# Column maxima by one-column stationaries on TensorE, bias rows made earlier, and new engine orders in a cross-attention + soft-MoE kernel

## The chip, the cores and the metric

One Trainium2 chip, one of its cores. The metric is device microseconds of one launch, the median of three runs. The engines are TensorE (PE, its weight loads shown as PEld), VectorE (DVE), ScalarE (ACT), GpSimd (POOL) and SyncE (SP), which issues all DMAs here.

## The reference

```
x   = x + xattn(layernorm(x), ctx, ctx, mask)          # 2x1024x256, 16 heads of 64, 154 keys
h   = layernorm(layernorm(x), norm_g, norm_b)
se  = layernorm(slot_embeds, slot_g, slot_b) * scale   # 16 experts x 64 slots = 1024 slots
logits   = einsum('bnd,esd->bnes', h, se)
dispatch = softmax(logits, axis=1)                     # over the 1024 tokens: column maxima
combine  = softmax(logits.reshape(B, N, -1), axis=-1)  # over the 1024 slots: row maxima
slots = einsum('bnd,bnes->besd', h, dispatch)
eout  = (gelu(slots @ Wg + bg) * (slots @ Wu + bu)) @ Wd + bd     # per expert, F = 512
x = x + einsum('bns,bso->bno', combine, eout)
```

All is float32. The kernel gets near this precision by splitting each operand into a "high" part of type fp32r and the rest, "low", and by summing three products (high·high, low·high, high·low).

## The kernel before

Each engine has its own list of events, and every list comes from one master order; the `LATER_*` tables move an event of one engine's list by so many places. PE follows the master order itself. The engines meet by semaphores only. Four stages follow one another: attention (0 to about 303 us), logits (to about 355), dispatch (to about 412) and experts (to about 508), then the combine.

**Logits.** For each of 16 tiles of 128 tokens: PE transposes the normed tile (`x2T`), ACT and DVE make its halves, PE multiplies with the slots (`L`, 12 matmuls), ACT copies the logits to SBUF (`lsb`), DVE keeps a running column maximum (`colmax`) and takes row maxima (`A`, `neg_amax`). For each batch b and half c, the column maxima are then brought to all rows: `MX` is four PE transposes of `colmax` and a DVE reduction to `nb`, whose column t holds the negated maxima of 128 slots, one a partition. DVE makes `diag`, four diagonal matrices (identity times `nb`, 128x512), and `MB` is one PE matmul ones·diag, a true float32 matmul that the trace shows as two records; DVE copies the result to `nb_b`.

**Dispatch.** For n = 0 to 15: POOL adds `nb_b` to the logits (`E`, into `disp_f` or `colmax`), ACT takes exp and the high half (`H`), DVE the low half, PE multiplies (`D`, 24 matmuls), DVE divides (`slot_f`), PE transposes (`sT`), and ACT and DVE make halves. Batch 0 has its maxima before the dispatch begins; batch 1's `MX` and `MB` stand at its opening.

**Weights.** Each expert has three pieces (0 gate, 1 up, 2 down), 512 KB each, in six places `w_raw`. ACT casts a piece to its high half (`W`, L786); POOL (L739) makes the low half of pieces 0 and 2, DVE (L983) that of piece 1. SP loads a piece into a place when the low half of the piece six before it has been made (L600).

**Experts.** For e: `GU` is 12 matmuls plus 2 that add bias rows from `b_row`; ACT takes gelu into `gate` and casts pieces 0 and 1 of expert e+2; DVE multiplies `hid` and makes the low half of piece (e+2, 1). `HT` is four PE transposes of `hid`, and ACT and DVE make `hT`. `EO` is 13 matmuls; DVE copies the result out as halves, and ACT casts piece 2. PE's order is GU(e+1), HT(e), EO(e-1), and a bank rule lets an accumulator be used again once DVE has freed the third one before it. `b_row` is cleared by DVE, filled by ACT (high) and DVE (low) between the last dispatch steps.

In the fences, the suffixed `wkq` and `w_second` are places that dispatch halves or weight halves use at that time.

## Time and profile before

| | |
|---|---|
| median of 3 runs | 572.33 us (571.97 to 572.97) |
| the profiled execution | 572.37 us, its span 570.6 us |
| PE busy | 537.8 us (94%) |
| DVE busy | 466.0 us (82%) |
| ACT busy | 395.1 us (69%) |
| POOL busy | 313.6 us (55%) |
| granted TensorE clock | 1.00 throughout |
| chain that ended last | PE 62%, DVE 16%, POOL 9%, ACT 7%, issue 6% |

Shares are averages over stages with different limits, so the table says only that PE is the main engine and that DVE stands in the chain for a sixth of the time. In a timeline row the number in brackets is how long the engine stood idle before it and who ended the wait. A row of several instructions is merged, so that its start and the next row's start give its pitch, while its own length has the last one's drain in it.

### The profile page before, as it was taken

The numbers are of one execution on the slowest core, as the hardware profiler recorded it, in microseconds if no ns is written. First come the engines' busy times: TensorE is split into PE (matmuls) and PEld (weight loads), VectorE is DVE, ScalarE is ACT, GpSimd is POOL, SyncE is SP. The second block draws the span as 40 slices with busy tenths as digits, with TensorE's granted clock in tenths as the row PEclk, the third lists the DMA queues.
The fourth block names the chain that finished last, engine by engine and source line by source line (L and its number), as shares of the span: only waits on it lengthen the run. The fifth ranks groups of instructions, "written<-read, shape, count | busy, mean of one in ns | idle before, by whom it ended". The sixth has DMA issues, their size and how long they took to land.

```text
span 570.6 us, 11928 instructions
## 1 busy us (share of the span) xinstructions
PE 537.8 (94%) x3877; PEld 499.5 (88%) x3877; DVE 466.0 (82%) x1354; ACT 395.1 (69%) x1073; POOL 313.6 (55%) x331
## 2 busy tenths in 40 slices
PE   5889999999999999999989998899979999999997
PEld 3778999999999989999977876799948787899997
DVE  7897878788797979898766997997788999985553
ACT  4976959698796959689663555578967676736662
POOL 7662554455445464453456766886498999920000
PEclk9999999999999999999999999999999999999999
DMA  8402000000030000000001433050268888516552
GB/s 262 169 1 75 2 2 2 1 2 1 2 93 2 2 2 0 3 1 2 1 2 74 184 149 148 38 191 18 82 204 277 273 284 271 180 38 184 167 169 73
DMA packets 29868, 51.78 MB, mean 91 GB/s; under 512 B 2037, under 2 KB 16465, under 8 KB 29681
## 3 DMA queue, kind: packets, MB, share of 16 engines
q1 hardware_dynamic: 29809, 51.04, 26.7%
q8 instruction: 32, 0.52, 0.4%
q14 instruction: 27, 0.22, 0.1%
HBM read 40.54 MB, written 10.49 MB: 89 GB/s over the span
## 4 chain that ended last, share of the span: by engine, by line
PE 62%; DVE 16%; POOL 9%; ACT 7%; issue 6%; DMA 0%; SPq 0%; POOLq 0%; ACTq 0%; DVEq 0%
PE ps L1453 8%; PE ps L1315 8%; PE ps L1516 7%; PE ps L1403 6%; PE ps L1485 6%; DVE w_gu_low L983 5%; PE ps L1436 5%; PE ps L1384 5%; PE ps L1415 4%; PE ps L1438 3%; PE ps L1575 2%; POOL prob L680 2%; ACT expo L828 2%; DVE eo_high L1263 1%; PE ps L1362 1%
## 5 line engine op out<-in xcount | busy, mean ns | idle before, releaser
L680 POOL TENSOR_TENSOR prob<-expo,prec 128x512 f32<-128x512 f32 x64 | 66.8, 1044 | 99.2 <-DVE prec L1100 97.9
L828 ACT ACTIVATE expo<-expo,nmin 128x154 f32<-128x154 f32 x256 | 106.2, 422 | 3.8 <-DVE nmin L1089 3.3
L1089 DVE CUSTOM_DVE_ANT_0 expo<-ps,maskb 128x154 f32<-128x154 f32 x256 | 69.1, 311 | 12.5 <-PE ps L1403 11.9
L1403 PE MATMUL ps<-kbd,qT_high 128*128 128x308 f32 x256 | 60.9, 321 | 0.3 <-ACT qT_high L754 0.3
L1109 DVE TENSOR_TENSOR pT_low<-ps,pT_high 128x512 fp32r<-128x512 f32 (+1 forms) x96 | 57.2, 595 | 4.1 <-ACT pT_high L842 3.6
L842 ACT CAST pT_high<-ps 128x512 fp32r<-128x512 f32 (+1 forms) x96 | 49.2, 515 | 15.2 <-PE ps L1415 11.5
L754 ACT ACTIVATE oT_high<-ps,bqv_c 128x256 fp32r<-128x256 f32 x64 | 29.9, 468 | 37.0 <-PE ps L1438 37.0
L828 ACT ACTIVATION_READ_ACCUMULATOR expo<-expo,nmin 128x1 f32 x256 | 50.1, 196 | 0.0
L739 POOL TENSOR_TENSOR wkq_low<-w_raw,wkq_high 128x1024 fp32r<-128x1024 f32 x15 | 48.1, 3208 | 1.5 <-ACT wkq_high L786 1.5
L739 POOL TENSOR_TENSOR w_gu_low<-w_raw,w_gu_high 128x1024 fp32r<-128x1024 f32 x17 | 41.8, 2465 | 11.8 <-ACT w_gu_high L786 11.8
L1403 PEld LDWEIGHTS ps<-kbd,qT_high 128*128 128x128 f32 x256 | 40.0, 190 | 0.9 <-issue 0.5
L983 DVE TENSOR_TENSOR w_gu_low<-w_raw,w_gu_high 128x1024 fp32r<-128x1024 f32 x14 | 37.6, 2683 | 2.7 <-ACT w_gu_high L786 2.7
L1403 PE MATMUL ps<-kbd,qT_low 128*128 128x308 f32 x128 | 39.0, 305 | 0.0
L1415 PE MATMUL ps<-ident,prob 128*128 128x128 f32 x256 | 38.4, 272 | 0.0
L1453 PE MATMUL ps<-wvo_high,oT_high 128*128 128x256 f32 x128 | 36.8, 287 | 0.0
L1453 PE MATMUL ps<-wvo_high,oT_low 128*128 128x256 f32 x128 | 36.2, 283 | 0.0
L1453 PE MATMUL ps<-wvo_low,oT_high 128*128 128x256 f32 x128 | 35.9, 281 | 0.0
L945 ACT CAST comb<-ps 128x512 fp32r<-128x512 f32 x32 | 17.3, 591 | 25.7 <-PE ps L1575 25.7
L971 DVE SCALAR_TENSOR_TENSOR oT_low<-ps,bqv_c,oT_high 128x256 fp32r<-128x256 f32 x64 | 30.4, 474 | 5.8 <-ACT oT_high L754 5.1
L1315 PE MATMUL ps<-eo_high,comb 128*128 128x256 f32 x256 | 34.6, 287 | 0.4 <-issue 0.4
L867 ACT COPY lsb<-ps 128x512 f32<-128x512 f32 x32 | 17.2, 589 | 25.2 <-PE ps L1485 25.2
L1315 PEld LDWEIGHTS ps<-eo_high,comb 128*128 128x128 f32 x256 | 31.7, 191 | 0.6 <-issue 0.6
(239 smaller groups left out, 1775.6 us busy)
## 6 DMA issues: line engine op xcount, KB each, us to landing
logits_dram<-lsb SPq DMA_DIRECT2D x16, 512.0 KB, 2.6
w_raw<-in_L_ffn_Wg_dram SPq DMA_DIRECT2D x16, 512.0 KB, 4.2
w_raw<-in_L_ffn_Wu_dram SPq DMA_DIRECT2D x16, 512.0 KB, 4.4
...
```

The lines of the kernel that those rows point to most:

```text
L680: pool.tensor_tensor(prob[:, n % 2, :, heads, :], expo[:, n % 2, pp, :, :, 0:P], prec[:, n % 2, pp].unsqueeze(3).to_broadcast([P, 2, 2, P] ...
L739: pool.tensor_tensor(low, w_raw[:, i % RAW].rearrange("p (k n) -> p k n", k=KD if w == 0 else FT), high, ALU.subtract).then_inc(low_made(e ...
L828: ins = act.activation(row, row, ACT.Exp, scale=-1.0, bias=nmin[:, n % 2, pp, j, h:h + 1], accum_out=psums[:, n % 2, pp, j, h:h + 1])
L842: act.copy(pT[0][0:rows, n % 2, 2 * t:2 * t + tiles], ps[0:rows, NS + k % NT, 0:tiles * 2 * P].rearrange("p (t n) -> p t n", t=tiles))\
L983: dve.tensor_tensor(low, w_raw[:, i % RAW].rearrange("p (k n) -> p k n", k=KD if w < 2 else FT), high, ALU.subtract).then_inc(low_made(e, ...
L1089: ins = dve.tensor_tensor_reduce(out=expo[:, n % 2, pp, j, h, :], in0=ps[:, s % NS, h * SK:(h + 1) * SK], in1=maskb[:, (2 * (n // QUADS) + ...
L1109: dve.tensor_tensor(pT[1][0:rows, n % 2, 2 * t:2 * t + tiles], ps[0:rows, NS + k % NT, 0:tiles * 2 * P].rearrange("p (t n) -> p t n", t=ti ...
L1315: ins = pe.matmul(dst[:, 0:D], combT[s][:, i % 2, t], eo[m][:, i // TB, t], start=(first and r == 0 and t == parts[0]), stop=(last and r = ...
L1403: ins = pe.matmul(dst, qT[s][:, n % 2, pp, j * P:(j + 1) * P], kbd[:, b, m, p, :], start=(r == 0), stop=(r == 2))
L1415: ins = pe.transpose(ps[:, NS + k % NT, (2 * h + j) * P:(2 * h + j + 1) * P], prob[:, n % 2, j, 2 * t + h, 0:P], ident[:])
L1453: ins = pe.matmul(dst[:, 0:D], oT[s][:, p, j * P:(j + 1) * P], wo[m][:, p], start=(p == 0 and r == 0), stop=(p == PAIRS - 1 and r == 2))
L1516: ins = pe.matmul(dst[:, 0:DN], disp[s][n % 3][:, i], x2[m][:, b * TB + i], start=(r == 0 and i == 0), stop=(r == 2 and i == TB - 1))
```

## The change

Four things:

1. `diag` and `ones` are gone. `MB` is four matmuls of 128 columns: the stationary is one column of `nb`, repeated 128 times by its access pattern, and the moving operand is the identity.
2. `b_row` has a place of its own in SBUF. POOL clears it in the logits; ACT and DVE fill it after step 9 of the dispatch, in place of its very end.
3. In the opening of the dispatch both transposes of batch 1 stand ahead of `D(0)`.
4. The tables that shift events are new, among them those of the experts.

The pieces of code below stand, in this order, on POOL (clearing `b_row`), on DVE (`MX`, then the event that cleared `b_row`) and on PE (`MB`).

```diff
-A_LATE = 4
+A_LATE = 3
-FIRST_AT = {9: [('C', 0)], 10: [('C', 1)], 11: [('C', 2)], 12: [('W', 0, 0)], 13: [('B', 0), ('W', 0, 1), ('gelu',)], 14: [('W', 0, 2), ('B', 1), ('W', 1, 2)]}
+FIRST_AT = {6: [('B', 1)], 9: [('C', 0)], 10: [('C', 2), ('C', 1)], 12: [('W', 0, 0)], 13: [('W', 0, 1), ('W', 0, 2), ('gelu',)], 14: [('W', 1, 2)]}
 SLOTS_HEAD = [
-    ("H", 0), ("MX", 1, 0), ("D", 0), ("H", 1), ("MX", 1, 1), ("MB", 1, 0),
+    ("H", 0), ("MX", 1, 0), ("MX", 1, 1), ("D", 0), ("H", 1), ("MB", 1, 0),
 ]
...
 LATER_EXPERTS_DVE = {
-    "HT": -2, "GU": -1, "C": -0.5,
+    "HT": -2, "C": -0.5, ("EO", 2): -1,
 }
...
-    b_row = sb(ex, "b_row", [P, BW], F32R)
+    b_row = nc.alloc_sbuf_tensor_at("b_row", [P, BW], F32R, offset=b_row_at)
...
+            elif ev == ("B", 0):
+                pool.wait_ge(acc_free, ATT_END)
+                pool.memset(b_row[:].bitcast(F32), 0.0).then_inc(b_zeros, 1)
...
-                part_nb = nb[:, 4 * c:4 * c + 4]
-                dve.tensor_reduce(part_nb, acc(no).rearrange("p (t n) -> p t n", t=4), AX, ALU.max, negate=True)\
-                    .then_inc(acc_free, 1)
-                wait_used(dve, ev)
-                dve.tensor_tensor(diag[:], ident[:].unsqueeze(1).to_broadcast([P, 4, P]),
-                                  part_nb.unsqueeze(2).to_broadcast([P, 4, P]), ALU.mult).then_inc(diag_ready, 1)
+                dve.tensor_reduce(nb[:, 4 * c:4 * c + 4], acc(no).rearrange("p (t n) -> p t n", t=4), AX, ALU.max,
+                                  negate=True).then_inc(acc_free, 1)
...
-                dve.wait_ge(d_shift, B * ST)
-                dve.wait_ge(d_lst, 16 * TILES)
-                dve.memset(b_row[:].bitcast(F32), 0.0)
...
-                pe.wait_ge(diag_ready, 2 * b + c + 1)
-                pe.matmul(dst, ones[:], diag[:].rearrange("p t n -> p (t n)"), start=True, stop=True)\
-                    .then_inc(acc_full, 1)
+                wait_used(pe, ("MX", b, c))
+                for t in range(4):
+                    ins = pe.matmul(dst[:, t * P:(t + 1) * P], nb[:, 4 * c + t:4 * c + t + 1].to_broadcast([P, P]),
+                                    ident[:], start=True, stop=True)
+                ins.then_inc(acc_full, 1)
```

DVE where the dispatch opens, from the low half of step 0 on; before:

```order
L1215 TENSOR_TENSOR disp_low<-disp_f_62,disp_high 128x1024
L1200 TENSOR_REDUCE nb<-ps 128x4
L1203 TENSOR_TENSOR diag<-ident,nb 128x512
L1221 RECIPROCAL den<-ps 128x1
L1222 TENSOR_SCALAR slot_f<-ps,den 128x256
L1215 TENSOR_TENSOR wkq_low<-ps,wkq_high 128x1024
L1200 TENSOR_REDUCE nb<-ps 128x4
L1203 TENSOR_TENSOR diag<-ident,nb 128x512
L1208 COPY nb_b<-ps 128x512
```

The same place of DVE now:

```order
L1214 TENSOR_TENSOR disp_low<-disp_f_62,disp_high 128x1024
L1202 TENSOR_REDUCE nb<-ps 128x4 x2
L1220 RECIPROCAL den<-ps 128x1
L1221 TENSOR_SCALAR slot_f<-ps,den 128x256
L1214 TENSOR_TENSOR wkq_low<-ps,wkq_high 128x1024
L1207 COPY nb_b<-ps 128x512
```

Both reductions now stand ahead of step 0's division, and nothing stands between a reduction and what PE waits for.

DVE in the experts, one period and the start of the next; before:

```order
L1250 TENSOR_TENSOR hid<-ps,gate 128x512
L983 TENSOR_TENSOR w_gu_low<-w_raw,w_gu_high 128x1024
L969 TENSOR_TENSOR hT_low<-ps,hT_high 128x512
L1263 CAST eo_high<-ps 64x256 x2
L1266 TENSOR_TENSOR eo_low<-ps,eo_high 64x256 x2
L1250 TENSOR_TENSOR hid<-ps,gate 128x512
```

The same place now:

```order
L973 TENSOR_TENSOR hT_low<-ps,hT_high 128x512
L1247 TENSOR_TENSOR hid<-ps,gate 128x512
L986 TENSOR_TENSOR w_gu_low<-w_raw,w_gu_high 128x1024
L1260 CAST eo_high<-ps 64x256 x2
L1263 TENSOR_TENSOR eo_low<-ps,eo_high 64x256 x2
L973 TENSOR_TENSOR hT_low<-ps,hT_high 128x512
```

`hT_low(e-1)` now precedes `hid(e)` and the weight half; it followed both.

ACT at the end of the dispatch, from step 13's halves of slots on; before:

```order
L893 CAST sT_high<-ps 128x2x64 x2
L902 ACT_TABLE_LOAD
L902 ACTIVATE csum<-csum 128x1
L786 CAST wkq_high<-w_raw 128x1024
L893 CAST sT_high<-ps 128x2x64 x2
L906 CAST b_row<-b_raw 16x1280
L786 CAST wkq_high<-w_raw 128x1024
L786 CAST w_second_high<-w_raw 128x1024 x2
```

The same place now, with the cast of piece (0, 2) in the first row:

```order
L790 CAST wkq_high<-w_raw 128x1024
L897 CAST sT_high<-ps 128x2x64 x2
L906 ACT_TABLE_LOAD
L906 ACTIVATE csum<-csum 128x1
L790 CAST wkq_high<-w_raw 128x1024
L897 CAST sT_high<-ps 128x2x64 x2
L790 CAST w_second_high<-w_raw 128x1024 x2
```

The bias cast has left this place, and the two down pieces come one place earlier each.

## Rows read from the trace of the kernel before

**Rows 1.** Windows: length, then busy us of PE, PEld, DVE, ACT, POOL, clock, DMA.

```profile
368.00:412.00 44.00, 44.00 (x368) 43.92 (x367) 36.94 (x80) 36.66 (x63) 27.62 (x13) 1.00 0.25 86
...
436.00:494.00 58.00, 55.59 (x316) 46.75 (x316) 56.58 (x71) 40.69 (x53) 58.00 (x21) 1.00 0.84 271
```

**Rows 2.** Timeline of PE where the dispatch opens: start, us, instruction, [idle before <-releaser].

```profile
361.99 1.10 PE L1502 MATMUL ps<-diag,ones 128*128 128x512 f32 x2 [0.90 <-DVE diag L1203]
...
367.12 1.10 PE L1502 MATMUL ps<-diag,ones 128*128 128x512 f32 x2 [1.15 <-DVE diag L1203]
```

**Rows 3.** Timeline of DVE: `diag` in the logits, then where the dispatch opens.

```profile
333.32 0.69 DVE L1203 TENSOR_TENSOR diag<-ident,nb 128x512 f32<-128x512 f32 x1
...
359.37 2.47 DVE L1203 TENSOR_TENSOR diag<-ident,nb 128x512 f32<-128x512 f32 x1
...
364.20 2.77 DVE L1203 TENSOR_TENSOR diag<-ident,nb 128x512 f32<-128x512 f32 x1
```

**Rows 4.** Timeline of POOL where the dispatch opens.

```profile
358.90 5.17 POOL L728 TENSOR_TENSOR disp_f<-lsb,nb_b 128x1024 f32<-128x1024 f32 x2 [1.25 <-DVE disp_low L1215]
364.03 2.39 POOL L728 TENSOR_TENSOR colmax<-lsb,nb_b 128x1024 f32<-128x1024 f32 x1
```

**Rows 5.** Timeline of PE in the logits.

```profile
337.29 1.02 PE L1502 MATMUL ps<-diag,ones 128*128 128x512 f32 x2
338.15 0.38 PE L1469 MATMUL ps<-ident,x2f 128*128 128x128 f32 x2
...
345.25 0.72 PE L1485 MATMUL ps<-wkq_high,x2T_high 128*128 128x512 f32 x2 [0.28 <-DVE x2T_low L969]
```

**Rows 6.** Timeline of PE from expert 0 to the first combine.

```profile
415.78 0.73 PE L1546 MATMUL ps<-b_row,b_pick 128*128 128x512 f32 x2 [0.94 <-DVE b_row L1243]
...
419.12 0.73 PE L1541 MATMUL ps<-w_second_low,sT_high 128*128 128x512 f32 x2 [1.46 <-DVE w_second_low L983]
...
428.77 0.36 PE L1560 MATMUL ps<-b_row,b_pick 128*128 128x256 f32 x1 [1.06 <-DVE hT_low L969]
...
507.89 1.84 PE L1315 MATMUL ps<-eo_high,comb 128*128 128x256 f32 x14
```

**Rows 7.** Timeline of POOL at the start of the experts.

```profile
406.55 4.77 POOL L739 TENSOR_TENSOR w_gu_low<-w_raw,w_gu_high 128x1024 fp32r<-128x1024 f32 x2 [9.16 <-ACT w_gu_high L786]
...
414.72 3.26 POOL L739 TENSOR_TENSOR wkq_low<-w_raw,wkq_high 128x1024 fp32r<-128x1024 f32 x1 [0.34 <-ACT wkq_high L786]
417.94 3.37 POOL L739 TENSOR_TENSOR w_second_low<-w_raw,w_second_high 128x1024 fp32r<-128x1024 f32 x1
```

**Rows 8.** Timeline of ACT and of DVE: the bias rows.

```profile
412.44 1.26 ACT L906 CAST b_row<-b_raw 16x1280 fp32r<-16x1280 f32 x1
...
414.15 1.58 DVE L1243 TENSOR_TENSOR b_row<-b_raw,b_row 16x1280 fp32r<-16x1280 f32 x1 [1.08 <-ACT b_row L906]
```

**Rows 9.** Timeline of DVE, one expert's period.

```profile
455.97 0.68 DVE L969 TENSOR_TENSOR hT_low<-ps,hT_high 128x512 fp32r<-128x512 f32 x1
...
458.33 0.69 DVE L1250 TENSOR_TENSOR hid<-ps,gate 128x512 f32<-128x512 f32 x1
458.94 2.82 DVE L983 TENSOR_TENSOR w_gu_low<-w_raw,w_gu_high 128x1024 fp32r<-128x1024 f32 x1
```

**Rows 10.** Timeline of POOL, the same period.

```profile
458.25 2.42 POOL L739 TENSOR_TENSOR w_gu_low<-w_raw,w_gu_high 128x1024 fp32r<-128x1024 f32 x1
460.62 3.40 POOL L739 TENSOR_TENSOR wkq_low<-w_raw,wkq_high 128x1024 fp32r<-128x1024 f32 x1
```

**Rows 11.** Timeline of PE, the same period.

```profile
456.74 0.36 PE L1560 MATMUL ps<-b_row,b_pick 128*128 128x256 f32 x1 [0.24 <-DVE hT_low L969]
```

**Rows 12.** Timeline of ACT, the same period.

```profile
456.10 0.60 ACT L912 ACTIVATE gate<-ps 128x512 f32<-128x512 f32 x1 [1.78 <-PE ps L1546]
...
458.49 0.60 ACT L754 ACTIVATE hT_high<-ps 128x512 fp32r<-128x512 f32 x1
```

**Rows 13.** Tile `w_raw` in the experts, last line of the answer.

```profile
DMA to landing us min/median/max: 3.2/4.2/5.9
```

More of the change, by code:

```diff
@@ L86 @@
 SLOTS_HEAD = [
-    ("H", 0), ("MX", 1, 0), ("D", 0), ("H", 1), ("MX", 1, 1), ("MB", 1, 0),
+    ("H", 0), ("MX", 1, 0), ("MX", 1, 1), ("D", 0), ("H", 1), ("MB", 1, 0),
 ]
-LOGITS_AT = {8: [('MX', 0, 0)], 10: [('MB', 0, 0)], 11: [('MX', 0, 1)], 13: [('E', 0), ('MB', 0, 1)], 14: [('E', 1)], 15: [('E', 2)]}
+LOGITS_AT = {3: [('B', 0)], 8: [('MX', 0, 0)], 10: [('MB', 0, 0)], 11: [('MX', 0, 1)], 13: [('E', 0), ('MB', 0, 1)], 14: [('E', 1)], 15: [('E', 2)]}
 LATER_SLOTS_ACT = {
     "GU": 3.5, ("E", 0): 4, ("E", 1): 4, ("E", 2): 7, "sT": 2, ("W", 0, 1): -0.5, ("E", 15): 1,
-    ("W", 1, 0): -1, ("GU", 1): 3, "E": 0.5, ("D", 1): 1, ("E", 14): 1.5,
+    ("W", 1, 0): -1, ("GU", 1): 3, "E": 0.5, ("D", 1): 1, ("E", 14): 1.5, ("E", 13): -1.5, ("W", 0, 2): -0.5,
 }
 LATER_SLOTS_DVE = {
-    "GU": 3.5, "L": 1, "A": 4, "E": -1, ("C", 2): 0.5, "H": 0.5, ("E", 15): 0.5, ("D", 1): -2, ("L", 13): 3,
-    ("W", 0, 2): -4, ("W", 0, 0): 4,
+    "GU": 3.5, "L": 1, "A": 4, "E": -3, ("C", 2): 0.5, "H": 0.5, ("E", 15): 0.5, ("D", 1): -2, ("L", 13): 3,
+    ("W", 0, 2): -4, ("W", 0, 0): 4, ("H", 3): 1.5, "x2T": -0.5, ("W", 1, 0): 1, ("E", 9): -2.5,
 }
 LATER_SLOTS_POOL = {
-    "E": 1.5, ("C", 0): 1, ("L", 14): -4, ("L", 13): 0.5, "L": 0.5, ("C", 1): 2, ("E", 8): 3.5, "MB": -1,
-    ("W", 0, 1): 0.5, ("E", 9): 0.5, ("E", 2): 0.5, ("H", 0): 1, ("H", 2): 1, ("GU", 1): -0.5,
[3 rows of a table added]
 }
 LATER_EXPERTS_ACT = {
-    "C": 2, ("EO", 14): -0.5,
+    "C": 2, ("EO", 14): -0.5, "CO": 2,
 }
 LATER_EXPERTS_DVE = {
-    "HT": -2, "GU": -1, "C": -0.5,
+    "HT": -2, "C": -0.5, ("EO", 2): -1,
 }
@@ L299, in program @@
     ident16 = sb(top, "ident16", [P, P], BF16)
-    ones = sb(top, "ones", [P, P])
     x1 = sb(top, "x1", [P, TILES, D])
@@ L379, in program @@
     nb = sb(lg, "nb", [P, ST])
-    diag = sb(lg, "diag", [P, 4, P])
     slot_f = sb(lg, "slot_f", [P, 2, D])
+    b_row_at = -(-nc.sbuf_base // 32) * 32
     lg.close()
@@ L469, in program @@
     l_full, l_ready, amax_ready, colmax_ready = sem("l_full"), sem("l_ready"), sem("amax_ready"), sem("colmax_ready")
-    diag_ready = sem("diag_ready")
     d_shift, d_exp, d_high, d_low = (sem(s) for s in ("d_shift", "d_exp", "d_high", "d_low"))
+    b_pick_ready, b_zeros = sem("b_pick_ready"), sem("b_zeros")
     w_high, gate_low, up_low, down_low, b_high, b_low = (sem(s) for s in (
@@ L904, in step @@
                 act.wait_ge(d_bias, 48)
-                act.wait_ge(const_dve, 3)
+                act.wait_ge(b_zeros, 1)
                 act.copy(b_row[0:E], b_raw[:]).then_inc(b_high, 1)
@@ L974, in _ @@
         dve.memset(eps[:], EPS)
-        dve.memset(mhalf[:], -0.5)
-        dve.memset(ones[:], 1.0).then_inc(const_dve, 1)
+        dve.memset(mhalf[:], -0.5).then_inc(const_dve, 1)
         def weight_low(e, w):
@@ L1195, in step @@
                 wait_done(dve, ev)
-                if (b, c) != (0, 0):
-                    wait_done(dve, ("MB", (2 * b + c - 1) // 2, (c + 1) % 2))
-                part_nb = nb[:, 4 * c:4 * c + 4]
-                dve.tensor_reduce(part_nb, acc(no).rearrange("p (t n) -> p t n", t=4), AX, ALU.max, negate=True)\
-                    .then_inc(acc_free, 1)
-                wait_used(dve, ev)
-                dve.tensor_tensor(diag[:], ident[:].unsqueeze(1).to_broadcast([P, 4, P]),
-                                  part_nb.unsqueeze(2).to_broadcast([P, 4, P]), ALU.mult).then_inc(diag_ready, 1)
+                if b:
+                    wait_done(dve, ("MB", 0, c))
+                dve.tensor_reduce(nb[:, 4 * c:4 * c + 4], acc(no).rearrange("p (t n) -> p t n", t=4), AX, ALU.max,
+                                  negate=True).then_inc(acc_free, 1)
             elif ev[0] == "MB":
@@ L1234, in step @@
             elif ev == ("B", 0):
-                dve.wait_ge(d_shift, B * ST)
-                dve.wait_ge(d_lst, 16 * TILES)
-                dve.memset(b_row[:].bitcast(F32), 0.0)
-                dve.tensor_tensor(b_pick[:], ident[:, 0:E], ident[:, 32:32 + E], ALU.add).then_inc(const_dve, 1)
+                dve.wait_ge(se_ready, ST)
+                dve.tensor_tensor(b_pick[:], ident[:, 0:E], ident[:, 32:32 + E], ALU.add).then_inc(b_pick_ready, 1)
             elif ev == ("B", 1):
-                dve.wait_ge(const_dve, 3)
+                dve.wait_ge(b_pick_ready, 1)
+                dve.wait_ge(b_zeros, 1)
                 dve.wait_ge(b_high, 1)
```

3 rows, old and new, of the table LATER_SLOTS_POOL are left out of this document.

## The prediction

> **What bounds the kernel now.** I read the chain that ended last first, then the windows stage by stage, then the timelines of all engines where PE stands idle. In the dispatch PE is busy for 44.00 of 44 us [rows 1], so a microsecond won before it goes straight through it. In the experts PE is busy for 55.59 of 58, DVE for 56.58 and POOL for 58.00 of 58: POOL never rests [rows 1]. One period there is 5.7 us: 2.36 from `hT_low` to `hid`, 0.61 to the weight half, 2.74 until the next `hT_low` can start [rows 9].
>
> Where the time of DVE's weight half goes is seen by laying DVE over POOL. It starts at 458.94 while POOL is in an instruction that ends at 460.62; DVE ends at 461.76, 1.13 after that boundary, and POOL's next one takes 3.40 instead of 2.42, 0.98 more [rows 9, 10]. So the two take turns by whole instructions: DVE waits for POOL's boundary, then POOL waits 1.1. `diag` shows the same: 0.69 alone, 2.47 and 2.77 beside POOL [rows 3], the last ending 0.6 after POOL's boundary at 366.4 [rows 4]. The Trainium skill says it in "SBUF — State Buffer", section "SBUF: two separate sides": whichever of a two-SBUF-input DVE operation and a GpSimd operation starts first keeps the shared port pair for its whole length. By that rule, the rows agree.
>
> Hence a period of two POOL lows and one DVE low is 2.37 + 2.22 + 1.13 = 5.7 in whatever order DVE does its list, and DVE's own wait is elastic. What the order does set is how far behind that beat PE runs. Before, PE's `EO` waits for `hT_low`, which stands behind the weight half: 0.24 us idle each period [rows 11].
>
> **The change part by part.** The sum is made on the profiled execution: span 570.6 us, 572.37 in all, 0.04 above the median of the runs.
>
> *Opening.* PE waits 0.90 and 1.15 us for `diag` [rows 2]. Now `MB` needs only `nb`. Both transposes are done before `D(0)`, both reductions of 0.7 us pass while `D(0)` runs for 3 us, and both `MB`s find `nb` ready. What is late next is step 1's low half on DVE, about 363.2, wanted in the third pass of `D(1)` at 364. It fits. Gain 2.05; at least 0.9 if only one wait goes.
>
> *MB itself.* The old one streams 512 columns in two records, 337.29 to 338.15, 0.86 us [rows 5]. The new one streams the same columns in eight pieces of 128. Below: 0.86, or somewhat less if the access pattern helps, which nothing shows. Above: the record of two 128-column transposes is 0.38 long, 0.19 each [rows 5]; eight unhidden ones would be 1.52, 0.66 more. All four `MB`s lie on PE's path, so the cost is between 0 and 2.6. I take 0.05 each, 0.2, since the columns stream alike and weight loads pass beside matmuls elsewhere here.
>
> *Logits.* Two `diag`s of 0.7 us leave a DVE that is nearly full; PE's wait of 0.28 goes [rows 5], and a part of the issue time around it. Gain 0.3 to 0.6; I take 0.4. POOL's clearing of `b_row`: DVE's took 1.1 us and POOL's of kbd is alike; it stands while POOL would wait for ACT, and delays `x2f` by about 0.5 with 1.5 to spare. Nothing; 0.5 at most if that cover is gone. The dispatch thus starts 2.05 + 0.4 − 0.2 = 2.25 us earlier.
>
> *Inside the dispatch.* ACT gets the bias cast, 1.26, DVE the subtraction, 1.58 [rows 8]. The windows leave ACT 7.3 and DVE 7.1 us idle in 44 [rows 1], the halves are made 2 to 3 us ahead of their matmuls in the middle, and the gap closes again before the end. The subtraction has two SBUF inputs, so it can wait for POOL's instruction of 2.4 us [rows 4], 4 in all; that still fits. DVE no longer has the fourth late row maximum. Cost 0 taken. At the end ACT's list is dense (three combine exps, E(13) to E(15), pieces): high halves 13 and 15 come only 0.2 and 0.6 us ahead. Bounds −0 to +2.5.
>
> *From dispatch to experts.* POOL makes the first lows: 406.55 for two, then one, then 3.26 and 3.37, ending at 421.3 [rows 7]. Three things stretch that: waits for ACT's casts, the subtraction of `b_row` (1.58, rows 8), and DVE's weight half. Now ACT has no bias cast there and both down pieces are cast earlier; the subtraction is gone. POOL starts at about 404.5 and makes five lows at 2.4 with one turn for DVE: 404.5 + 11.9 + 1.1 = 417.5, 3.8 earlier. PE's waits of 0.94 (bias) goes [rows 6], and those for POOL's lows in experts 1 and 2 remain, with their ends 3.7 earlier.
>
> *DVE's new order.* `hT_low(0)` no longer stands behind a weight half, so `EO(0)` starts at about 423.9, not 428.77 [rows 6]: 4.9 earlier. Call X the end of DVE's weight half in expert e. Then DVE copies `EO` (1.76), makes `hT_low` (0.6) and `hid` (0.7): `hid` is ready at X + 3.1, and the next request waits for POOL, X + 5.7. PE now waits in `HT(e)` for `hid`, and not in `EO`. The new wait of DVE is `hT_low` for ACT: gelu starts 456.10 and `hT_high` ends 459.09, 3.0 later [rows 12]; gelu can start with `hid`, X + 3.1, so `hT_high` is there at X + 6.1 and is wanted at X + 5.7 + 1.8 = X + 7.5. Slack 1.4. Queued behind that wait are `hid`, the weight half and the copies of `EO`, for which PE waits.
>
> Laid out by these durations, X is 424.5, 430.9, 436.6 for pieces (3,1), (4,1), (5,1), then every 5.7 us, the tenth later at 493.6. The old last one is at 496.0. So the beat is 2.3 to 2.4 earlier, and PE stands nearly 3 us nearer to it than before, which makes `EO(3)` 5.1 earlier. The end gives part of that back: `HT(15)` needs `hid(15)`, behind two copies of `EO` and one `hT_low` more: 493.6 + 1.8 + 0.6 + 0.7 + 1.8 + 0.6 + 0.7 = 499.8. From there `HT`, half a combine transpose, `EO(14)`, `EO(15)` are 4.1 us, so the first combine starts at 503.9 and not at 507.89 [rows 6]: 4.0 earlier, 4.2 if the dispatch has the full 2.25.
>
> *Combine.* Nothing in it is moved. **Sum:** 572.37 − 4.2 = 568.2 us; against the median, 568.1.
>
> **The rivals.**
>
> A. *PE breaks away from the beat.* If ACT's cast of piece (2,2) is a little later than I have it (0.35 us between POOL's start and DVE's request), DVE gets its turn one POOL instruction earlier. The beat is then 2 us earlier from expert 2 on. For: the margin is small. Against: POOL is full and has the same work. 568.1 − 2.2 = 565.9.
>
> B. *Only the opening pays.* PE stays tied to POOL's stream, which in the end hangs on ACT's casts and on the loads: `GU` and `EO` wait for POOL's halves in place of DVE's. For: POOL 58.00 of 58 [rows 1]. Against: its halves are done about 4 us before PE needs them. Gain 2.25 and some 0.3: 569.8.
>
> C. *The dispatch gets crowded, or `MB` is dear.* High halves 12 to 15 each late by 0.5 (2.0), or the upper bound of `MB`. For: 0.2 us of slack. 570.4.
>
> D. *Slower: `hid` behind ACT.* DVE now does nothing until ACT has cast two pieces, and these wait for loads. A load may start when DVE's low half two experts earlier is made, and takes 4.2 in the median, 5.9 at most [rows 13]. I have piece (6,1) land only 0.25 us before its cast. It decides from a landing of 4.4 + 0.25 + 1.4, about 6 us: then `hT_high` comes after X + 7.5, DVE misses POOL's boundary, and a period costs 0.5 more. Eleven such periods are 5.5, less 4.2: 573.6. For: PE runs earlier than its data did before, while the places `w_raw` are as many. Against: only the longest landing seen reaches it.
>
> E. *It doesn't do what it says.* If repeated columns as stationary ran at a slower pace than any row here, `MB` could cost back the 2.05; that ends at 570 to 572.5 and shares C's chance.
>
> **How the numbers follow.** Forecast 0.50, its own range 566.8 to 569.3. A 0.15, B 0.14, C with E 0.13, D 0.08. The measurement tells about 0.2%, 1.1 us, from no change: faster is below 571.2. Faster: all of the forecast, A and B, and most of C: 0.86. Same: the rest of C, and D where half the periods are late: 0.07. Slower 0.07. The range for 8 in 10 is 565.5 to 571.0; it has the forecast, A, B and C, and leaves out D and the tails.
>
> **What would show it.** Opening: no idle before the two `MB`s, each 0.85 to 1.0 us, and the dispatch's first steady step 2.0 to 2.5 us earlier. DVE: `nb` rows of 0.7, no two-input operation in the opening besides step 0's. Transition: POOL's five lows without a gap, ending near 417.5; no wait of PE for `b_row`. Experts: period 5.7, POOL full; PE's idle of 0.2 to 0.4 before `HT` (waiting for `hid`), none before `EO`. First combine near 503.9. I am wrong if `MB` takes 1.2 or more, if PE waits in the dispatch for `disp_high` or `wkq_high`, if the period isn't 5.7, or if DVE's idle before `hT_low` grows over the 1.4 of slack.

## The result and the profile after

| | before | changed | ratio, 95% interval |
|---|---|---|---|
| first chip | 572.44 us (571.97 to 572.97, 4 runs) | 567.46 us (567.09 to 569.12, 4 runs) | 0.9918 [0.9906, 0.993] |
| a later chip, the changed kernel again | 572.2 us (572.11 to 573.18, 11 runs) | 568.19 us (567.08 to 569.55, 6 runs) | 0.9927 [0.9915, 0.9938] |

The forecast was 568.1 us with a range of 565.5 to 571.0. The profiled execution took 567.2 us, its span is 565.4, 5.2 less than before. The page gives PE 537.4 us busy (95%), DVE 453.9, ACT 395.7, POOL 312.7, and the chain of what ended last:

```profile
PE 62%; DVE 14%; POOL 10%; ACT 7%; issue 5%; DMA 2%; SPq 1%; POOLq 0%; ACTq 0%; DVEq 0%
```

DVE's share fell from 16 to 14%, and there is a new 2% of DMA, of which more below. The windows that answer to [rows 1], with the same columns:

```profile
368.00:412.00 44.00, 44.00 (x363) 43.70 (x363) 35.59 (x79) 39.32 (x67) 28.79 (x13) 1.00 0.29 95
436.00:494.00 58.00, 56.09 (x324) 47.29 (x324) 56.37 (x75) 41.14 (x52) 56.76 (x20) 1.00 0.79 260
```

PE is still busy in all of the dispatch. In the experts POOL is no longer at 58.00 of 58. PE has 0.5 us more here, but that belongs to one event of this execution (told below); a second profile of the same kernel, without it, has 55.24:

```profile
436.00:494.00 58.00, 55.24 (x316) 45.84 (x315) 56.87 (x73) 39.56 (x51) 56.72 (x21) 1.00 0.75 256
```

**Opening.** PE's timeline, which answers to [rows 2]; the waits for `diag` are gone, and nothing stands before either `MB`:

```profile
356.48 1.91 PE L1491 MATMUL ps<-ident,colmax 128*128 128x128 f32 x8 [2.16 <-DVE colmax L1189]
358.04 2.05 PE L1515 MATMUL ps<-x_high,disp_high 128*128 128x258 f32 x8
359.90 1.15 PE L1515 MATMUL ps<-x_low,disp_high 128*128 128x258 f32 x8
...
361.86 1.05 PE L1500 MATMUL ps<-ident,nb 128*128 128x128 f32 x8
...
365.62 1.05 PE L1500 MATMUL ps<-ident,nb 128*128 128x128 f32 x8
...
366.65 1.21 PE L1515 MATMUL ps<-x_high,wkq_high 128*128 128x258 f32 x8
```

From the first transposes of batch 1 to `D(2)` it is 10.17 us; before it was 11.10 (357.12 to 368.22). That is 0.93 less, not the 2.05 of the forecast. The reason is in the pitch (the time from one group's start to the next one's): eight matmuls of `D(0)` take 1.86 us (358.04 to 359.90), and other groups of eight about 1.0. The windows of this stretch (clock in the third column from the end) say why:

```profile
350.00:356.40 6.40, 4.32 (x19) 3.17 (x17) 3.40 (x6) 4.08 (x7) 6.40 (x4) 1.00 0.35 145
356.40:358.00 1.60, 1.52 (x8) 1.55 (x9) 1.59 (x1) 1.51 (x2) 0.62 (x1) 0.54 0.74 300
358.00:359.80 1.80, 1.80 (x10) 1.80 (x9) 1.30 (x3) 1.71 (x3) 1.53 (x1) 0.50 0.00 0
```

After the idle 2.16 us in front of the transposes the granted clock is at half, that is 1.2 GHz, until `D(0)`'s first eight matmuls are through, and then it goes back to 2.4 GHz (0.97 in the mean from 359.80 to 362.00). Before had 1.00 there, although the idle 2.16 us is the same. A second profile of the changed kernel (span 566.2) had 1.00 throughout, and the same stretch, 357.06 to 365.65, takes 8.59 us:

```profile
357.06 1.07 PE L1491 MATMUL ps<-ident,colmax 128*128 128x128 f32 x8 [2.16 <-DVE colmax L1189]
...
365.65 1.20 PE L1515 MATMUL ps<-x_high,wkq_high 128*128 128x258 f32 x8
```

**From dispatch to experts.** POOL's timeline, which answers to [rows 7]. Five low halves without a gap, the last ending at 417.63 (before 421.27); from the start of the first it is 12.79 us, before 14.72:

```profile
404.84 4.76 POOL L743 TENSOR_TENSOR w_gu_low<-w_raw,w_gu_high 128x1024 fp32r<-128x1024 f32 x2 [9.11 <-ACT w_gu_high L790]
409.56 4.77 POOL L743 TENSOR_TENSOR wkq_low<-w_raw,wkq_high 128x1024 fp32r<-128x1024 f32 x2
414.30 3.38 POOL L743 TENSOR_TENSOR w_second_low<-w_raw,w_second_high 128x1024 fp32r<-128x1024 f32 x1
417.63 5.74 POOL L743 TENSOR_TENSOR w_gu_low<-w_raw,w_gu_high 128x1024 fp32r<-128x1024 f32 x2
```

**To the combine.** PE's timeline, which answers to [rows 6]. No wait for `b_row`, and the first `EO` at 423.83 without one; the first combine is 5.13 earlier than 507.89:

```profile
415.48 0.74 PE L1540 MATMUL ps<-w_second_low,sT_high 128*128 128x512 f32 x2 [0.66 <-DVE w_second_low L986]
...
421.06 0.73 PE L1540 MATMUL ps<-w_gu_low,sT_high 128*128 128x512 f32 x2 [0.77 <-POOL w_gu_low L743]
...
423.83 0.36 PE L1559 MATMUL ps<-b_row,b_pick 128*128 128x256 f32 x1
...
502.76 1.82 PE L1312 MATMUL ps<-eo_high,comb 128*128 128x256 f32 x14
```

**One period** of DVE, which answers to [rows 9], and the PE row of it, which answers to [rows 11]: PE now waits for `hid`, in `HT`, and `hT_low` is ahead of `hid`.

```profile
438.67 0.69 DVE L973 TENSOR_TENSOR hT_low<-ps,hT_high 128x512 fp32r<-128x512 f32 x1
439.27 0.68 DVE L1247 TENSOR_TENSOR hid<-ps,gate 128x512 f32<-128x512 f32 x1
439.87 2.67 DVE L986 TENSOR_TENSOR w_gu_low<-w_raw,w_gu_high 128x1024 fp32r<-128x1024 f32 x1
```

```profile
440.10 0.63 PE L1552 MATMUL ps<-ident,hid 128*128 128x128 f32 x4 [0.38 <-DVE hid L1247]
```

In that run one thing more happened, at 450. ACT's cast of a down piece waited 1.75 us for its load, POOL waited 0.97 for that cast, and DVE, which asked in just that gap, made its weight half at once, in 1.22 us. In the two periods before it had taken 2.67 and 2.80, and in the next it took 2.38:

```profile
451.26 1.22 DVE L986 TENSOR_TENSOR w_gu_low<-w_raw,w_gu_high 128x1024 fp32r<-128x1024 f32 x1
```

```profile
450.34 1.05 ACT L790 CAST wkq_high<-w_raw 128x1024 fp32r<-128x1024 f32 x1 [1.75 <-DMA w_raw<-in_L_ffn_Wd_dram]
```

```profile
451.47 3.29 POOL L743 TENSOR_TENSOR wkq_low<-w_raw,wkq_high 128x1024 fp32r<-128x1024 f32 x1 [0.97 <-ACT wkq_high L790]
```

From there all is 1.4 us ahead of the beat (the rhythm of 5.7 us). Call this a slip. The second profile has none, and from the end of POOL's five lows to the first combine it needs 86.50 us (416.61 to 503.11) where the first needs 85.13. The first profile thus holds a loss of about 1.6 (the clock) and a gain of about 1.4 (the slip), which hide each other. The table cuts the span of each profile into stretches that add up to it. The first row, all work ahead of the second logits tile, is not touched by the change, and yet it differs from one execution to another.

| us, profiled executions | before | changed, first | changed, second |
|---|---|---|---|
| start to the transposes of the second logits tile | 302.58 | 302.71 | 303.26 |
| from there to the first transposes of batch 1 (logits) | 54.54 | 53.77 | 53.80 |
| first transposes of batch 1 to `D(2)` | 11.10 | 10.17 | 8.59 |
| `D(2)` to POOL's first low half | 38.33 | 38.19 | 38.17 |
| five low halves | 14.72 | 12.79 | 12.79 |
| from there to the first combine | 86.62 | 85.13 | 86.50 |
| first combine to the end of the span | 62.71 | 62.64 | 63.09 |
| span | 570.6 | 565.4 | 566.2 |

### The profile page after: what moved, and what is told of

It is laid out like the page before. It is cut to its first block, busy times and chain, and to the rows that moved or that the text cites. A ratio compares the mean times of both kernels' runs of the same rounds, so it can differ in the third digit from the quotient of the medians.

```text
span 565.4 us, 11969 instructions
## 1 busy us (share of the span) xinstructions
PE 537.4 (95%) x3901; PEld 502.5 (89%) x3901; DVE 453.9 (80%) x1348; ACT 395.7 (70%) x1073; POOL 312.7 (55%) x332
## 4 chain that ended last, share of the span: by engine, by line
PE 62%; DVE 14%; POOL 10%; ACT 7%; issue 5%; DMA 2%; SPq 1%; POOLq 0%; ACTq 0%; DVEq 0%
PE ps L1450 8%; PE ps L1312 8%; PE ps L1482 7%; PE ps L1515 6%; PE ps L1400 6%; DVE w_gu_low L986 5%; PE ps L1433 5%; PE ps L1381 5%; PE ps L1412 4%; PE ps L1435 3%; PE ps L1574 2%; POOL prob L680 2%; ACT expo L832 2%; DVE eo_high L1260 2%; POOL w_gu_low L743 1%
## 5 line engine op out<-in xcount | busy, mean ns | idle before, releaser
L743 POOL TENSOR_TENSOR w_gu_low<-w_raw,w_gu_high 128x1024 fp32r<-128x1024 f32 x17 | 44.7, 2632 | 11.8 <-ACT w_gu_high L790 11.7
L743 POOL TENSOR_TENSOR wkq_low<-w_raw,wkq_high 128x1024 fp32r<-128x1024 f32 x15 | 43.8, 2924 | 1.0 <-ACT wkq_high L790 1.0
L986 DVE TENSOR_TENSOR w_gu_low<-w_raw,w_gu_high 128x1024 fp32r<-128x1024 f32 x14 | 34.1, 2435 | 0.0
```

The costliest lines, as they stand in the source:

```text
L743: pool.tensor_tensor(low, w_raw[:, i % RAW].rearrange("p (k n) -> p k n", k=KD if w == 0 else FT), high, ALU.subtract).then_inc(low_made(e ...
L986: dve.tensor_tensor(low, w_raw[:, i % RAW].rearrange("p (k n) -> p k n", k=KD if w < 2 else FT), high, ALU.subtract).then_inc(low_made(e, ...
```

## The experiments

Each kernel was timed beside the kernel before on its chip; ratios are against that. Three chips were used for the experiments, and the kernel before had medians of 572.93 (experiments 1 to 4), 572.57 (5 to 8) and 572.2 (9 to 12).

### 1 and 2. DVE's new order in the experts, alone and undone

The kernel before with only this table changed, and the changed kernel with the old one:

```diff
 LATER_EXPERTS_DVE = {
-    "HT": -2, "GU": -1, "C": -0.5,
+    "HT": -2, "C": -0.5, ("EO", 2): -1,
 }
```

> The kernel before, with one edit: the new table of DVE's events in the experts (hT_low(e-1) ahead of hid(e) and the weight half). Theory T (POOL and DVE take turns by whole instructions, the period is 5.7 us in any order, and DVE's order sets only how far behind that beat PE runs): PE's wait moves from EO to HT and PE comes closer to the beat, the end gives part back; 1.0 to 2.0 us faster than before, period still 5.7. Rival R (the experts gained only because POOL's first five low halves came earlier; DVE's order is worth nothing): within 0.3 us of before. Rival D (hid stands behind ACT's casts): slower by 1 us or more.

> The changed kernel, with DVE's old table in the experts. T: EO waits for hT_low behind the weight half again, 1.0 to 2.0 us slower than the changed kernel (about 569), period 5.7, POOL's first five lows as early as in the changed kernel. R: within 0.3 us of the changed kernel (567.5).

Alone it measured 572.26 us (571.96 to 573.1, 11 runs), ratio 0.9994 [0.9985, 1.0003]; undone, 567.57 (567.22 to 568.61, 4 runs), 0.9913 [0.9899, 0.9926]. So the order is worth nothing that can be measured, and the expectation of 1 to 2 us fell. The traces say why. In experiment 1 the last weight half of DVE ends at 497.21, 1.24 later than the old 495.97, since one item more stands ahead of it; but the first combine comes 10.30 us behind that and not 11.92:

```profile
507.51 1.84 PE L1315 MATMUL ps<-eo_high,comb 128*128 128x256 f32 x14
```

From POOL's five lows to the combine it takes 86.51 with the new order and 86.62 with the old; on top of the rest of the change it is 86.50 (second profile) and 86.66 (experiment 2). PE is nearer to DVE's beat, and the end gives it back.

Experiment 1's trace also tells what the fall of the clock costs the kernel before. Here it fell too (windows of PE's opening):

```profile
356.80:359.00 2.20, 2.10 (x10) 2.14 (x11) 2.18 (x2) 2.11 (x3) 0.94 (x2) 0.52 0.55 222
359.00:361.00 2.00, 2.00 (x14) 2.00 (x13) 1.97 (x2) 1.76 (x2) 2.00 (x1) 0.67 0.00 0
```

```profile
362.22 1.02 PE L1502 MATMUL ps<-diag,ones 128*128 128x512 f32 x2
...
366.91 1.10 PE L1502 MATMUL ps<-diag,ones 128*128 128x512 f32 x2 [0.78 <-DVE diag L1203]
...
368.01 1.22 PE L1516 MATMUL ps<-x_high,wkq_high 128*128 128x258 f32 x8
```

The first `MB` no longer waits for `diag` and the second waits 0.78. From the first transposes to `D(2)` it is 11.12 us with the fall, and 11.10 in the profile of before, without it. The old kernel's waits for DVE take up what the slow matmuls lose. The 1.31 us of `D(1)`'s first pass here (362.73 to 364.04) stands behind an `MB` that waited for nothing; it will matter in experiment 3.

### 3. The one-column `MB` alone

The kernel before with the new `MX` and `MB` on PE and DVE, all tables old:

```diff
-                pe.matmul(dst, ones[:], diag[:].rearrange("p t n -> p (t n)"), start=True, stop=True)\
-                    .then_inc(acc_full, 1)
+                for t in range(4):
+                    ins = pe.matmul(dst[:, t * P:(t + 1) * P], nb[:, 4 * c + t:4 * c + t + 1].to_broadcast([P, P]),
+                                    ident[:], start=True, stop=True)
+                ins.then_inc(acc_full, 1)
```

> The kernel before, with only the column maxima done by one-column stationaries (no diag, no ones; all orders as before). T: the two waits of 0.90 and 1.15 us at the opening mostly go, MB takes 0.89 instead of 0.86; but MX(1,1) still stands behind D(0), so a part of a wait stays, and PE may lose some clock there; 1.0 to 2.5 us faster than before. Rival (diag was hidden, the gain at the opening came from the new order of MX): under 0.5 us.

569.92 us (569.48 to 570.67, 5 runs), ratio 0.9955 [0.9941, 0.9969]: 3.0 us less, more than the 1.0 to 2.5 expected. The profile had 1.00 throughout: 8.62 us from the first transposes to `D(2)` (357.13 to 365.75), 2.48 less than before. The brackets of the two waits were 2.05 of it. Most of the rest is that a wait costs PE more than its bracket, since the bracket begins when the last matmul in front has drained, and without a wait the next one starts before that. From the second transposes to the first `MB` it was 1.51 us and is 0.43, 1.08 less for a bracket of 0.90; from the third pass of `D(1)` to the second `MB` it was 2.27 (364.85 to 367.12) and is 0.98, 1.29 less for a bracket of 1.15. The rows of before, and those of this run (where the transposes' row is 0.60 us long, too, but `MB` starts 0.43 behind their start):

```profile
360.48 0.60 PE L1494 MATMUL ps<-ident,colmax 128*128 128x128 f32 x4
```

```profile
360.48 0.60 PE L1490 MATMUL ps<-ident,colmax 128*128 128x128 f32 x4
360.91 1.06 PE L1499 MATMUL ps<-ident,nb 128*128 128x128 f32 x8
```

The matmuls behind the waits were not slower. `MB` and the first pass of `D(1)` together take 1.89 us before (361.99 to 363.88), 1.82 in experiment 1, where nothing waited in front of them, and 1.86 here.

The logits, too, are 0.75 us shorter: 53.79 us from the second tile's transposes (303.34) to the first of batch 1, against 54.54. Most of it lies in front of the two `MB`s there. The second one in the kernel before, from the transposes ahead of it:

```profile
344.59 0.38 PE L1469 MATMUL ps<-ident,x2f 128*128 128x128 f32 x2
...
348.15 1.02 PE L1502 MATMUL ps<-diag,ones 128*128 128x512 f32 x2
```

and here:

```profile
345.12 0.38 PE L1465 MATMUL ps<-ident,x2f 128*128 128x128 f32 x2
...
348.12 1.05 PE L1499 MATMUL ps<-ident,nb 128*128 128x128 f32 x8
```

That is 3.56 and 3.00 us; for the first one it is 3.30 (333.99 to 337.29) and 3.00 (334.78 to 337.78). What follows `D(2)` is as before.

### 4. The bias rows at their old place

```diff
-FIRST_AT = {6: [('B', 1)], 9: [('C', 0)], ... 14: [('W', 1, 2)]}
+FIRST_AT = {9: [('C', 0)], ... 14: [('B', 1), ('W', 1, 2)]}
```

> The changed kernel, with the bias rows' cast (ACT) and subtraction (DVE) put back to the end of the dispatch, ahead of the cast of piece (1,2); b_row is still cleared by POOL in the logits. T: ACT's later casts come 1.2 us later and the subtraction takes a turn of 1.4 us from POOL, so POOL's first five lows end 1.5 to 2.5 us later and PE waits for them; 1.0 to 2.5 us slower than the changed kernel (568.5 to 570). Rival (the bias rows were covered, what made POOL's lows earlier was the earlier dispatch alone): within 0.3 us of 567.5.

569.59 us (568.6 to 569.9, 5 runs), ratio 0.9941 [0.9929, 0.9954], in the expected 568.5 to 570. POOL's second down piece waits 0.28 us for ACT and takes 3.33 where it takes 2.4 in the changed kernel; the five lows take 14.01 us instead of 12.79, and from POOL's first low to the first combine it is 100.53 us where experiments 7 and 8 have 99.27 and 99.29:

```profile
412.04 3.33 POOL L743 TENSOR_TENSOR wkq_low<-w_raw,wkq_high 128x1024 fp32r<-128x1024 f32 x1 [0.28 <-ACT wkq_high L790]
```

```profile
413.16 0.73 PE L1545 MATMUL ps<-b_row,b_pick 128*128 128x512 f32 x2 [0.16 <-DVE b_row L1240]
```

The wait for `b_row` itself is 0.16 us. So it is not that wait that made the bias rows dear, but what ACT's cast and DVE's subtraction did to POOL's chain.

### 5 and 12. Matmuls in the wait

The changed kernel with nine matmuls of 512 bf16 columns, whose result nobody reads, in PE's wait before the first transposes of batch 1:

```diff
+                if (b, c) == (1, 0):
+                    for _ in range(9):
+                        pe.matmul(ps[:, 4, :], ident16[:], ident16[:].unsqueeze(1).to_broadcast([P, 4, P]),
+                                  start=True, stop=True)
                 pe.wait_ge(colmax_ready, TB * (b + 1))
```

> The changed kernel, with nine 128x512 bf16 matmuls into an unused bank right after the last logits matmul, in the 2.16 us in which PE waits for the last colmax; their result is never read. In the changed kernel's profile the transposes and the first pass of D(0) behind this wait ran at a lower clock (8 transposes in 1.56 us, 8 matmuls in 1.86 us instead of about 1.0). Theory C (the clock fell because PE stood idle for 2.16 us): no slow stretch, 1.0 to 1.6 us faster than the changed kernel (about 566.2). Rival (a disturbance of that one execution, or not caused by the wait): same as the changed kernel, 567.5.

> The changed kernel with nine filler matmuls in the wait before the first transposes of batch 1, the same as before, beside the changed kernel on one chip. If the idle 2.16 us brings the fall of the clock, all of its runs have a mean clock of 1.000 and the median is 0.5 to 1.5 us below the changed kernel's. If the fall is chance and not that wait, some of its runs have 0.997 as well and the medians are within 0.3.

566.93 us (566.79 to 567.47, 4 runs), ratio 0.9905 [0.989, 0.992], and on another chip, beside the changed kernel, 566.93 (566.82 to 567.48, 4 runs), 0.9905 [0.9892, 0.9918].

```profile
354.07 2.12 PE L1491 MATMUL ps<-ident 128*128 128x512 bf16 x9
356.30 1.09 PE L1495 MATMUL ps<-ident,colmax 128*128 128x128 f32 x8
```

On one chip it is 1.3 us below the changed kernel's 568.19; against the first chip's 567.46 it is 0.5, less than the 1.0 to 1.6 that were expected.

All 8 runs had a mean clock of 1.000. A mean of 0.996 or 0.997 is what the profiles have in which the clock fell at this place (the first of the changed kernel, experiments 1, 4, 6, 7 and 8), and it is counted as that fall in the other runs. Of the changed kernel's 10 runs on both chips 3 had 1.000 and 7 had 0.996 or 0.997; of the kernel before it was 21 of 35. So the idle 2.16 us is what lets the clock fall, in about two thirds of the runs of either kernel.

The price is read best from the traces. From the first transposes of batch 1 to `D(2)` it is 10.10 to 10.17 us in the five profiles of the new opening with the fall (the first of the changed kernel, experiments 4, 6, 7 and 8) and 8.59 to 8.63 in four without it (the second of the changed kernel, experiments 2, 5 and 12), so the fall costs the new opening about 1.5 us. The spans of whole runs show it less sharply, since the work ahead of the logits ends 1.1 us earlier or later from one profile to another (302.35 to 303.45): kernel by kernel, the mean span of the runs with the fall is longer by 0.7 us (the changed kernel, 566.5 against 565.9) to 1.6 (experiment 7). In the old opening it costs nothing that can be told: 570.98 against 570.73 in the kernel before, and in experiment 1 the 8 runs with it are 0.4 us shorter in the mean than the 3 without.

### 6. No turns between POOL and DVE

DVE's up-weight low halves from expert 2 on are replaced by a memset of the same size; the low part of these weights is thus left out of the result.

```diff
                 if e + 2 < E:
-                    weight_low(e + 2, 1)
+                    dve.wait_ge(w_high, i + 1)
+                    dve.memset(low.bitcast(F32), 0.0).then_inc(low_made(e + 2, 1)[0], 1)
```

> The changed kernel, where for experts 2 to 15 DVE's low half of the up weights is left out and a memset of the same place to zero stands for it, so that DVE has no operation with two SBUF inputs there (the low part of Wu is missing from the result). Theory T (DVE and POOL take turns): each POOL low takes 2.4 us, none 3.3; POOL has rests, the period is PE's own 5.3 to 5.5 us, PE hardly waits for hid; 2.5 to 4.5 us faster than the changed kernel (about 564). Rival (POOL's 3.3 us lows come from the DMA traffic or from what they write, not from DVE): POOL's lows stay at 3.3, period 5.7, gain under 1 us.

562.04 us (561.47 to 562.6, 4 runs), ratio 0.9817 [0.9803, 0.983]: 5.4 below the changed kernel's 567.46, more than the 2.5 to 4.5 expected (the changed kernel was not timed on this chip). All of POOL's low halves from expert 2 on take 2.4 us, and PE has no idle time left:

```profile
461.80 2.42 POOL L743 TENSOR_TENSOR w_gu_low<-w_raw,w_gu_high 128x1024 fp32r<-128x1024 f32 x1 [0.45 <-ACT w_gu_high L790]
```

```profile
436.00:490.00 54.00, 54.00 (x320) 47.16 (x319) 39.81 (x75) 40.34 (x52) 49.69 (x21) 1.00 0.84 275
```

The period is 5.22 us and no longer 5.70. What paces the experts is the turns, worth 6.0 us from the five lows to the combine (80.49 against 86.50; the memset is also 0.2 us shorter than the 1.13 of the subtraction it stands for), and behind them stands PE itself. A memset by DVE, without an SBUF input, made nobody wait.

### 7. The old tables of the logits and the dispatch

```diff
-A_LATE = 3
+A_LATE = 4
```

and the three `LATER_SLOTS_*` tables as before.

> The changed kernel, with the old tables of shifts for ACT, DVE and POOL from the logits to the first experts and A_LATE = 4; the places of the events in the master order are the new ones. T (in the dispatch PE bounds, so these shifts are covered but for the first casts of weights): slower than the changed kernel by 0 to 0.8 us (567.5 to 568.3). Rival (the searched shifts bring a good part of the gain): slower by over 1.5 us (569 or more).

568.36 us (566.83 to 568.76, 5 runs), ratio 0.9923 [0.991, 0.9935]. In its profile the clock fell too, and the three rows of the table above from the first transposes of batch 1 to the end of the five low halves are 10.13, 38.42 and 12.77 us, against 10.17, 38.19 and 12.79. The new tables bring 0.2 us, in the dispatch. The median, just over the expected 567.5 to 568.3, says no more than that, since four of the five runs had the fall.

### 8. The second transposes behind `D(0)` again

```diff
-    ("H", 0), ("MX", 1, 0), ("MX", 1, 1), ("D", 0), ("H", 1), ("MB", 1, 0),
+    ("H", 0), ("MX", 1, 0), ("D", 0), ("H", 1), ("MX", 1, 1), ("MB", 1, 0),
```

> The changed kernel, with MX(1,1) behind D(0) again. T: DVE's division of step 0 and low half of step 1 stand before its second reduction; MB(1,1) still finds nb ready, since it comes 3 us after; within 0.3 us of the changed kernel (567.5). Rival (the new place is needed): 0.5 to 1.2 us slower.

568.41 us (567.59 to 569.04, 5 runs), ratio 0.9928 [0.9916, 0.994]. By the number alone the rival would have it, 0.9 us over 567.5; the trace decides against it. From the first transposes to `D(2)` it is 10.12 us in its profile, in which the clock fell too, against 10.17: no difference. Four of its five runs had the fall, as had five of the six of the changed kernel on the later chip, whose median was 568.19.

### 9, 10 and 11. Fewer POOL halves; the changed kernel again

If the turns pace the experts, a gate half moved from POOL (2.4 us) to DVE (1.13 us) should take load from them. On top of experiment 5, for experts 5, 9 and 13 (in 10 for 4, 7, 10 and 13), with a semaphore of their own:

```diff
+                if e + 2 in GATE_LOW_DVE:
+                    weight_low(e + 2, 0)
                 if e + 2 < E:
                     weight_low(e + 2, 1)
...
-            if w != 1:
+            if w != 1 and (w or e not in GATE_LOW_DVE):
                 weight_low(e, w)
```

> The changed kernel with the nine filler matmuls, and with the low half of the gate piece of experts 5, 9 and 13 made by DVE, right ahead of that expert's up piece, in place of POOL. T (the experts are paced by what POOL and DVE do in turn: two POOL halves of 2.4 us and one DVE half of 1.13 a period, and a DVE half costs the pair 1.13 where a POOL half costs 2.4): three moved halves take up to 3 x 1.27 = 3.8 us from that stream, so the time is 1.5 to 3.8 us below the filler kernel's 566.9, that is 563.1 to 565.4. R (DVE, 53.0 of 54 us busy with its waits counted, becomes the bound, and PE waits for hid by the same 3 x 1.13 or more): 566.5 to 569.

> The same with the gate pieces of experts 4, 7, 10 and 13, one in three. T: up to 4 x 1.27 = 5.1 us less POOL stream, 562 to 565, and at least 0.5 below the kernel with three. R (DVE is the bound): not below the kernel with three, 566.5 to 570.

> The changed kernel word for word, for a direct comparison on one chip. Its time should be 567.0 to 567.2 where the granted clock stays at 1.00 throughout and 568.3 to 568.8 where the clock falls in the opening of the dispatch (mean clock 0.997), with 567.1 to 567.5 where the clock falls and DVE also slips one turn ahead by a late load. So the span of the runs with a mean clock of 1.000 should be 1 to 1.5 us below that of the others.

Three halves: 575.94 us (575.34 to 581.11, 6 runs), ratio 1.0084 [1.0055, 1.0113]. Four: 582.64 (581.79 to 582.86, 4 runs), 1.0175 [1.0162, 1.0188]. T (the load would fall) is refuted, and R (DVE as the bound) was far too small: against experiment 12 a moved half costs 3.0 us when three are moved and 3.9 when four are. The two longest runs with three, 578.09 and 581.11 us, also have the lowest mean clocks (0.988 and 0.982, the others 0.994). The timelines of DVE, POOL and PE in experiment 9, at the first of them:

```profile
432.15 5.68 DVE L992 TENSOR_TENSOR w_gu_low<-w_raw,w_gu_high 128x1024 fp32r<-128x1024 f32 x2
```

```profile
431.00 2.39 POOL L749 TENSOR_TENSOR wkq_low<-w_raw,wkq_high 128x1024 fp32r<-128x1024 f32 x1 [2.83 <-ACT wkq_high L796]
433.93 2.81 POOL L749 TENSOR_TENSOR w_gu_low<-w_raw,w_gu_high 128x1024 fp32r<-128x1024 f32 x1 [0.54 <-ACT w_gu_high L796]
436.71 3.35 POOL L749 TENSOR_TENSOR wkq_low<-w_raw,wkq_high 128x1024 fp32r<-128x1024 f32 x1
442.63 2.39 POOL L749 TENSOR_TENSOR w_gu_low<-w_raw,w_gu_high 128x1024 fp32r<-128x1024 f32 x1 [2.57 <-ACT w_gu_high L796]
```

```profile
437.88 0.74 PE L1552 MATMUL ps<-w_gu_low,sT_high 128*128 128x512 f32 x2 [1.00 <-DVE w_gu_low L992]
...
441.07 0.63 PE L1564 MATMUL ps<-ident,hid 128*128 128x128 f32 x4 [1.99 <-DVE hid L1253]
```

The two DVE halves are not one turn. The first gets its turn at 433.39, where POOL's ends; POOL asks at 433.93, and gets it before DVE's second half does, which starts only after 436.7. The two take 5.68 us and not 2.3; at all seven places of the two experiments they take 5.48 to 6.60. PE waits 1.00 for the gate half and 1.99 for `hid`, which together are the 3.0 of a moved half. Behind the second wait the clock is down, as the window shows (0.50 from 442 to 445):

```profile
442.00:448.00 6.00, 6.00 (x28) 5.29 (x28) 5.53 (x12) 3.05 (x4) 4.70 (x2) 0.75 0.94 306
```

ACT gets its work from PE late, and POOL waits 2.57 us for ACT, so that the load taken from it is lost as idle time.

Experiment 11 gave the second profile shown above. Its one run at 1.000 had 567.91 us, 0.7 more than expected, and the five others 567.08 to 569.55; their spans are 0.4 us longer in the mean, not 1 to 1.5. The profile of the run at 1.000 shows most of the reason: its logits began 0.55 us later than in the first profile (303.26 against 302.71), ahead of all that was changed. With one run on one side this kernel alone doesn't settle the price of the fall; the traces do.

## Why the prediction was right, point by point

- **The sum.** 568.1 was forecast, 567.46 and 568.19 measured. The parts of the mechanism were found where the forecast had them, but the total owes something to luck. Where the clock does not fall, the gain is about 5.5 us and not 4.2: experiments 5 and 12 have spans of 565.1, against 570.6. In experiment 12 the opening and the logits give 2.47 and 0.84, in place of the forecast's 2.25 for both with the four `MB`s taken off, and all that follows gives 2.2, in place of 1.95. The fall of the clock, which the forecast does not have, takes about 1.5 back in two runs of three.
- **Opening, 2.05.** The step "gain 2.05" was mis-sized, and one thing was missing from it. Without the fall of the clock the gain is 2.5 (experiment 3, and the second profile with 11.10 to 8.59): each wait cost 0.14 to 0.18 more than its bracket. With the fall it is 0.93. The forecast looked at a profile in which the clock stood at 1.00 and did not ask what the idle 2.16 us would cost once the waits that follow are gone.
- **`MB` at 0.05 more.** 0.89 us from its start to the transposes behind it, 0.86 before [rows 5]:

```profile
337.13 1.05 PE L1500 MATMUL ps<-ident,nb 128*128 128x128 f32 x8
338.02 0.38 PE L1466 MATMUL ps<-ident,x2f 128*128 128x128 f32 x2
```

  Right; the upper bound was never near, and the kernel before could have shown it. The bias rows of the experts are multiplied with `b_pick[:, e:e + 1]`, one column repeated 128 times as stationary (type fp32r), the row of [rows 11]. Its weight loads took 185 to 191 ns there, as those of the plain `ones` did (186 to 189); those of `nb` take 188 to 192. So "which nothing shows" was wrong, and rival E's condition could have been priced ahead of the run.
- **Logits, 0.4.** Measured from the transposes of the second tile to the first of batch 1 it is 54.54 us in the kernel before and in experiment 1, which have `diag`, and 53.67 to 53.80 in the other twelve profiles, which don't; experiment 3, where only `diag` and `MB` differ, has 53.79. So the reason given, that DVE is freed of `diag`, is shown, and the term was too small: 0.75. In absolute times this is hidden, since the work ahead of the logits ends anywhere from 302.35 to 303.45. Experiment 3 reaches batch 1's transposes at 357.13, as late as before with 357.12, because its logits began 0.76 later.
- **Dispatch, 0.** `D(2)` to POOL's first low is 38.17 to 38.19 us against 38.33. The slack of 0.2 us for high half 13 held; PE waited for nothing there.
- **POOL's five lows end at 417.5.** 417.63. The chain is 1.93 shorter, where the forecast's two numbers (start 2.05 and end 3.8 earlier) made it 1.75. The profile began 0.34 later than forecast, and the shorter chain made up for a part of it. Experiment 4 gives 1.2 of it to the place of the bias rows; the rest goes with the casts of the down pieces, which come one place earlier.
- **DVE's order.** `EO(0)` at 423.83 (forecast 423.9), the period 5.7, PE's waits in `HT` of 0.2 to 0.4, `hid` 3.09 after the weight half (3.1): all as laid out. "POOL full" is not quite so: with the new order it is busy for 56.7 of 58 (experiment 2, with the old order, has 58.00), since it waits 0.2 us for ACT's cast of the gate piece in every second period. That wait costs nothing, as DVE has the turn then. X of the last was to be 493.6; it is 493.96 and 494.00 in experiments 8 and 7, and 492.45 in the first profile, by the slip. The forecast's own lay-out left the order worth 0.2 (first combine 4.0 earlier, POOL's lows 3.8), and experiments 1 and 2 agree with that; the 1 to 2 us that were expected when they were sent read too much into the `EO(3)` that comes 5 us earlier.
- **First combine at 503.9.** 504.27 and 504.32 where the clock fell and nothing slipped (experiments 8 and 7), 503.11 where neither (second profile, whose logits began late) and 502.40 in experiment 12, 502.76 in the first profile.
- **Rivals.** A (PE gets ahead of the beat) happened in one profile, by a late load and not by the cast of piece (2, 2); it gave 1.4. D, that late loads hurt, did not happen: a load kept ACT waiting for 1.75 us at 450, and the gap that this made on POOL let DVE in and brought more than it cost. C is excluded by the dispatch, in which PE is busy for 44.00 of 44, and by `MB`. B's number is excluded by the five lows, which are 1.93 shorter. But its thought, that the experts pay only what POOL's stream gives, is what experiments 1 and 2 found: from the five lows on, DVE's order is worth 0.1 to 0.2.

The fastest kernel with the whole result is the changed one with the nine filler matmuls: 566.93 us against 568.19 on the same chip, with intervals of the ratios that just overlap (0.9905 [0.9892, 0.9918] and 0.9927 [0.9915, 0.9938]).
